# Attention: weigh and total steps placed one at a time by the planner, six slots for exponentials, and a later load of the output weights

## What is computed

```
x = x + 0.5 * ffn(layernorm(x))
x = x + attention(layernorm(x))
x = x + 0.5 * ffn(layernorm(x))

attention(X):                       # 16 heads of 32, causal, 2048 tokens, per batch of 2
    Xn = layernorm(X) * ln_g + ln_b
    Q, K, V = Xn @ Wq + bq, Xn @ Wk + bk, Xn @ Wv + bv
    scores = Q @ K.T / sqrt(32), -inf above the diagonal
    A = softmax(scores)
    return (A @ V) @ Wo + bo
```

## Time and profile before

| | us |
|---|---|
| median of 3 runs | 2569.63 (2569.61 to 2570.26) |
| the profiled execution | 2570.1 |
| its span of instructions | 2568.3 |
| TensorE busy in the span | 2478.6 (97%) |
| VectorE busy | 1770.7 (69%) |
| GpSimd busy | 1543.9 (60%) |
| ScalarE busy | 1465.2 (57%) |

### The profile page before, as it was taken

One profiled execution on the slowest core, in us unless ns is written; L12 is line 12 of the kernel. 1 busy time (PEld: TensorE's weight loads), 2 busy tenths in 40 slices (PEclk: granted clock), 3 DMA queues, 4 the chain that ended last, 5 costly groups with the idle time before them and its releaser, 6 DMA issues.

```text
span 2568.3 us, 39616 instructions
## 1 busy us (share of the span) xinstructions
PE 2478.6 (97%) x14559; PEld 1100.9 (43%) x14559; DVE 1770.7 (69%) x3016; ACT 1465.2 (57%) x2829; POOL 1543.9 (60%) x1604
## 2 busy tenths in 40 slices
PE   5899999999999999999999999999999999999998
PEld 3444444444443434333344434444333444444443
DVE  7866666667659594948486695858575866666665
ACT  6666666665225656566622256565655466666665
POOL 3467666764316767676442267676774467766775
PEclk9999999999999999999999999999999999999999
DMA  2012211121122020200231312020004301111101
GB/s 67 17 47 78 91 41 50 50 99 66 33 60 61 12 46 22 52 6 2 88 128 34 81 41 52 7 52 22 3 4 149 123 17 50 50 50 50 50 33 50
DMA packets 78017, 130.58 MB, mean 51 GB/s; under 512 B 19551, under 2 KB 24698, under 8 KB 77694
## 3 DMA queue, kind: packets, MB, share of 16 engines
q1 hardware_dynamic: 77822, 128.05, 16.2%
HBM read 68.23 MB, written 31.46 MB: 39 GB/s over the span
## 4 chain that ended last, share of the span: by engine, by line
PE 77%; POOL 6%; DVE 6%; ACT 4%; issue 2%; SPq 1%; DMA 0%; POOLq 0%; DVEq 0%; ACTq 0%
PE pp L97 59%; PE ps L97 17%; POOL sb L106 5%; ACT sb L103 4%; DVE sb L112 2%; DVE sb L118 1%; SPq L139 1%; PE ps L100 1%; POOL sb L109 1%; DVE sb L106 1%; PE pp L100 0%; DVE sb L115 0%; DMA sb<-sb 0%; DVE sb L109 0%; DVE sb L124 0%
## 5 line engine op out<-in xcount | busy, mean ns | idle before, releaser
L97 PE MATMUL pp<-sb,sb 128*128 128x512 f16 (+8 forms) x11230 | 2068.8, 420 | 32.6 <-DVE sb L112 14.4
L106 POOL TENSOR_TENSOR sb<-sb,sb 128x512 f32<-128x512 f32 (+7 forms) x1353 | 1490.9, 1127 | 993.2 <-PE pp L97 330.4
L97 PEld LDWEIGHTS pp<-sb,sb 128*128 128x128 f16 (+3 forms) x11230 | 799.8, 102 | 1068.5 <-issue 214.5
L97 PE MATMUL ps<-sb,sb 128*128 128x512 f16 (+8 forms) x2786 | 723.1, 348 | 26.8 <-DVE sb L112 13.6
L103 ACT ACTIVATE sb<-pp 128x512 f32<-128x512 f32 (+6 forms) x1035 | 521.2, 560 | 331.2 <-PE pp L97 317.3
L118 DVE TENSOR_REDUCE sb<-pp 128x1 f32<-128x512 f32 (+3 forms) x704 | 441.0, 667 | 150.2 <-PE pp L97 150.0
L103 ACT ACTIVATE sb<-sb 128x512 f16<-128x512 f32 (+4 forms) x513 | 326.0, 650 | 366.0 <-DVE sb L112 306.4
L112 DVE SCALAR_TENSOR_TENSOR sb<-pp,sb,sb 128x512 f32<-128x512 f32 x447 | 324.6, 746 | 151.5 <-PE pp L97 136.6
L112 DVE SCALAR_TENSOR_TENSOR sb<-ps,sb,sb 128x512 f32<-128x512 f32 x437 | 318.1, 747 | 154.7 <-PE ps L97 128.7
L97 PEld LDWEIGHTS ps<-sb,sb 128*128 128x128 f16 (+3 forms) x2786 | 251.3, 97 | 339.9 <-DVE sb L118 36.0
L103 ACT ACTIVATE sb<-ps 128x512 f32<-128x512 f32 (+5 forms) x473 | 262.7, 566 | 155.3 <-PE ps L97 123.2
(11 more groups left out here) (29 smaller groups left out, 373.3 us busy)
## 6 DMA issues: line engine op xcount, KB each, us to landing
sb<-sb SPq DMA_DIRECT2D x144, 128.0 KB, 2.4
sb<-L_attn_X SPq DMA_DIRECT2D x64, 256.0 KB, 3.4
sb<-xa SPq DMA_DIRECT2D x64, 256.0 KB, 4.2
sb<-xc SPq DMA_DIRECT2D x64, 256.0 KB, 3.4
xa<-sb SPq DMA_DIRECT2D x32, 256.0 KB, 2.0
xc<-sb SPq DMA_DIRECT2D x32, 256.0 KB, 4.4
out<-sb SPq DMA_DIRECT2D x32, 256.0 KB, 2.0
sb<-sb SPq DMA_DIRECT2D x48, 96.0 KB, 2.2
```

The costliest lines, as they stand in the source:

```text
L97: return self.e.matmul(*a, **k) if self.e else self
L106: return self.e.tensor_tensor(*a, **k) if self.e else self
```

## The change

The block of three is given up. The 240 weigh and total steps still come in one fixed sequence (weigh 0, weigh 1, then weigh k, total k-1, weigh k+1 for each even k), but each is a candidate of its own, and the planner tracks whether the array was last used by f16 matmuls ("row") or by 32-column ones ("col"). From "row" a weigh or total costs 100 ns and a penalty of 300 ns less a fifth of VectorE's backlog; from "col" it costs only its waits, less 0.11 of the smaller backlog of VectorE and ScalarE. The weights of the other costs change as well, among them that of max units by their lead. Scores may run 11 heads ahead of the next weigh (15 once no max unit is left), and those beyond eight get a penalty of 300 ns.

Slots are no longer counted round. `pick` takes the known slot that is released first: four slots up to step 15, six from step 16 (two new ones at C0 and C0 + 8192, where the projected keys of head groups 0 and 1 lay, free once these are stacked), and from step 120 the same six as before. An even step's slot is free after its pair's total, as before; an odd step's slot is free once its exponentials are weighed and added, head by head.

The load of Wo comes right behind total 119 (the C0 slots are in use until then), with a wait for it on SyncE's queue, and `wo_split` starts after step (3, 1, 4), n = 128. The rule by which additions go to VectorE is the same in effect (the first clause of `late`, four steps after the last rows; the second can't be true with its 1e9), and is now kept as a set.

```diff
 class Att: __init__
-        self.E = [... for x in [o + 8192 * i for i in range(NE)] + [QS0 + 98304, QS0 + 106496]]
+        self.E = [... for x in [o + 8192 * i for i in range(NE)] + [QS0 + 98304, QS0 + 106496, C0, C0 + 8192]]
-    def place(self, n):
-        ...
 order
-        m = 0
-        while m < N:
+        m, hold = 0, [None] * 8
+        def released(k):
+            if k is None:
+                return 0.0
+            if k % 2:
+                return max(added[k], weigh_end[k]) if k in added else None
+            return sum_end.get(k + 1)
+        def pick(n):
+            most = range(NE) if n < 16 else (0, 1, 2, 3, 6, 7) if n < 120 else range(6)
+            known = [(released(hold[i]), i) for i in most if released(hold[i]) is not None]
+            return min(known) if known else None
+        late, mode, where = False, "row", 0
+        line = [x for k in range(0, N, 2) for x in
+                [("total", k - 1) if x == "T" else ("weigh", k + int(x)) for x in '0T1'] if x[1] >= 0]
+        while line:
...
-            if ready and 4 * n + j < 4 * m + 8 + (4 if wide else 4):
+            if ready and 4 * n + j < 4 * m + 8 + (7 if wide else 3):
-                cand.append((max(pe, clear[i], rowed[steps[n][0:2]]) + 0.200000 * hunger + (0 if first else 0.000000), "score", i))
+                cand.append((max(pe, clear[i], rowed[steps[n][0:2]]) + 0.050000 * hunger + (0 if first else 300.000000), "score", i))
-                    hunger = max(dve - pe, 0) + 10000.000000 * (lead - 0.080000)
-                    cand.append((max(pe, clear[i]) + 0.200000 * hunger, "max", i))
+                    hunger = max(dve - pe, 0) + 6272.000000 * (lead - 0.096000)
+                    cand.append((max(pe, clear[i]) + 0.050000 * hunger, "max", i))
...
-            if n >= m + 2 and (m == 0 or m - 1 in added):
-                ...
-                cand.append((pe + idle + 2500.000000 - 1.000000 * min(max(dve - pe, 0), 2000), "stay", 0))
+            op, k = line[0]
+            can = k in added if op == "total" else 4 * n + j >= 4 * k + 4
+            if can:
+                ok = (max(added[k], inverted if steps[k][2] == 1 else 0.0) if op == "total" else
+                      max(exped[k, 3], kept if steps[k][2] == 0 else 0.0))
+                begin = max(ok, pe + (100.000000 if mode == "row" else 0))
+                cand.append((begin + (300.000000 - 0.200000 * min(max(dve - pe, 0), 2000) - 0.000000 * min(max(act - pe, 0), 2000)
+                                      if mode == "row" else
+                                      0.000000 - 0.110000 * min(max(min(dve, act) - pe, 0), 2000)), "stay", 0))
...
             if what == "stay":
-                seq = [("total", m - 1) if x == "T" else ("weigh", m + int(x)) for x in '0T1']
-                m += 2
+                seq = [line.pop(0)]
+                if op == "weigh":
+                    m = k + 1
+                elif k == 119:
+                    seq.append(("wo", None))
+                if mode == "row":
+                    pe += 100.000000
+                mode = "col"
...
-                      if steps[n] == (2, 1, 0):
-                          out.append(("wo",))
-                      if steps[n] == (2, 3, 0):
+                      if steps[n] == (3, 1, 4):
                           parts.extend(("wo_split", c) for c in range(KC))
 att_act, score
-            elif m >= 0:
-                e.wait_ge(*t.sum_done.at((b, m + 1 - m % 2)))
+            elif m % 2 == 0:
+                e.wait_ge(*t.sum_done.at((b, m + 1)))
             else:
+                e.wait_ge(*t.av_done.at((b, m)))
+                e.wait_ge(*(t.late_added.at((b, m, j // 2)) if m in t.late[b] else t.e_added.at((b, m, j))))
 att_sp, wo
+            e.wait_ge(*t.sum_done.at((b, 119)))
```

More of the change, by code:

```diff
@@ L1324, in __init__ @@
         self.banks = [Banks() for _ in range(B)]
-        self.late = [0] * B
+        self.late = [set() for _ in range(B)]
+        self.slots = {}
         self.late_added = p.sign("a_late_added")
         self.plan = [list(self.order(b)) for b in range(B)]
-    def place(self, n):
[L1331 to L1335, removed]
     def offset(self, n):
@@ L1418, in order @@
         total_units, total_scores = len(units), 4 * N
-        m = 0
-        while m < N:
+        m, hold = 0, [None] * 8
[13 more added lines that the diff above has]
+        while line:
             n, j = scored
-            slot = self.place(n)[1] if n < N else None
-            free = slot is None or slot < 0 or slot + 1 - slot % 2 in sum_end
+            free = n < N and (j or pick(n))
             wide = not units
@@ L1474, in order @@
                   pe = at + c / 2.4 + 3 + (57 if kt >= 4 * qt else 0)
-                  place, old = self.place(n)
-                  free = sum_end.get(old + 1 - old % 2, 0.0) if old is not None and old >= 0 else 0.0
+                  if j == 0:
+                      gone, slot = pick(n)
+                      self.slots[n] = slot, hold[slot]
+                      hold[slot] = n
+                  free = gone
                   act = max(act, pe + 235, free) + 0.833 * c + 52
@@ L1521, in order @@
                   out.append(ev)
+              elif what == "wo":
+                  out.append(("wo",))
               elif what == "weigh":
@@ L1529, in order @@
                   if n % 2:
+                      work, start = 4 * c, max(weigh_end[n - 1], exped[n, 3])
+                      if late and n >= late or max(dve, start) + 1.04 * work + 1000000000.000000 < max(pool, start) + 2.117 * work:
+                          self.late[b].add(n)
                       for h in range(4):
                           start = max(weigh_end[n - 1], exped[n, h])
-                          if self.late[b] and n >= self.late[b]:
+                          if n in self.late[b]:
                               dve = max(dve, start) + 1.04 * c + 32
@@ L1549, in order @@
                       inverted = max(dve, sum_end[n]) + 745
-        self.sum_up(out, parts, N - 1)
+        for k in range(N - 2 + 1, N, 2):
+            self.sum_up(out, parts, k)
         yield from out
@@ L1665, in att_pe @@
                 e.wait_ge(*t.inverted.at((b, *t.steps[n - 2][0:2], 0)))
-            e.wait_ge(*(t.late_added.at((b, n, 1)) if n >= t.late[b] else t.e_added.at((b, n, 3))))
+            e.wait_ge(*(t.late_added.at((b, n, 1)) if n in t.late[b] else t.e_added.at((b, n, 3))))
             for j in range(4):
-                k = e.matmul(RS[32 * j:32 * j + 32, off:512], p.ones[:, :], t.E[t.place(n - 1)[0]][:, j, off:512],
+                k = e.matmul(RS[32 * j:32 * j + 32, off:512], p.ones[:, :], t.E[t.slots[n - 1][0]][:, j, off:512],
                              start=kt == 1, stop=last)
@@ L1752, in att_dve @@
             n = at[0]
-            if n % 2 and n >= t.late[b]:
+            if n in t.late[b]:
                 add_steps(e, p, b, n, t.late_added)
@@ L1799, in att_pool @@
             n = at[0]
-            if n % 2 and n < t.late[b]:
+            if n % 2 and n not in t.late[b]:
                 add_steps(e, p, b, n, t.e_added, 1)
```

43 lines of the change are left out of this document (18 added, 25 removed).

## The result

The changed kernel takes 2537.95 us, the median of 4 runs (2537.59 to 2538.51), against 2569.95 us for the kernel before on the same chip: 32 us less, ratio 0.9874 with a 95% interval of 0.9857 to 0.9892. The forecast was 2540 us.

A forecast was written before the change was run, and what follows sets the result against it. TensorE, busy 97%, was taken as the bound, with 44 us of waits in each 504 us loop. Gains 6 + 11 - 5 + 0 + 2 + 1 = 15 us a batch, twice 30, gave 2570.1 - 30 = 2540 us; range 2512 to 2567.

The forecast's parts named there:

- 6 + 11 + 2 + 1: Attention loops, us gained a batch: 6 six slots, 11 single steps, 2 Wo's split, 1 start and last rows.
- second kind: Stretches with max units: full banks make loads wait, about 17 us a batch; single steps were to remove 11.
- first kind: Stretches without max units: weighs wait for their own exponentials, about 13 us a batch; six slots were to gain 6.
- GpSimd as next limit: Stretches without max units: GpSimd's four additions a pair, 4.96 us, hold the period at about 5.0 us, not 4.60.
- 105 blocks at 0.20 us: Attention loops: 25 more 32-column blocks a batch than 80, each 0.20 us for changing form, 5 us lost.
- the ends (0.10 to 0.33): Bounds in us on the price of changing to 32-column form and back, taken as 0.20.
- The estimate of 0.33 us a block: Price of a 32-column block by the Trainium skill's 166 ns latency; 25 blocks would cost 8 us, not 5.
- 2 of 6 us were to go: ScalarE's copies for the splits: 6 us of waits a batch, 2 covered by exponentials up to eleven heads ahead.
- waits go nearly whole: Rival, attention loops: slots and single steps fill each full bank, 27 us a batch gained, 2516 us; chance 0.17.
- Slots waiting for GpSimd in place of the total: Rival, stretches without max units: period stays 5.48 us, gain only 7 us a batch, 2556 us; chance 0.18.
- VectorE as the true bound: Rival, stretches with max units: VectorE bounds, savings return as changes of form, no measurable change, 2570 us; chance 0.05.
- Slower by changes of form, from 180 blocks on: Rival, attention loops: from 180 blocks a batch the change loses; at 240 blocks 2594 us; chance 0.08.

The follow-up runs named there:

- singles: Single steps with the changed kernel's cost weights, but four slots up to step 120 and early Wo load as in the kernel before; 2552.46 us.
- wolate: The kernel before with only the late load of Wo and its late split; 2575.74 us, ratio 1.0018 to the kernel before.
- oddtotal: The changed kernel, but odd steps' slots also wait for their pair's total, six slots kept; 2537.15 us, 148 blocks a batch.
- pen150: The changed kernel with the planner's penalty for leaving f16 matmuls at 150 ns instead of 300; 2604.45 us, 184 blocks.
- pen1000: The changed kernel with the planner's penalty for leaving f16 matmuls at 1000 ns instead of 300; 2949.23 us, 107 blocks.
- lowlate: The changed kernel with GpSimd's eight subtractions for the splits moved to steps 148 to 155; 2537.45 us, ratio 0.9872 to the kernel before.

## Why the prediction was right, step by step

**The place and the sum.** The loops were to shrink by 15 us a batch; between the same two matmuls they shrank by 16.5 and 16.3 us. TensorE's records stayed in number. The place, the kinds of gain and loss and the next limit were right. That the sum came out right to 2 us is luck in part, because two errors in it met: 10 us too few of waits gone, 10 us too few for blocks.

**The waits.** Forecast were 20 us of 44 gone a batch (6 + 11 + 2 + 1); 30 went. The term of the second kind was too small. I gave single steps 11 of 17 us and left them nothing of the first kind; singles shows that they take 27 us with four slots, blocks without max units included. A block of three had to wait for its last exponential in line, while single steps let TensorE score in between. So the two parts overlap, and the split of the gain by kinds (6 for slots, 11 for steps) doesn't hold. The slots' own share was 4 us a batch in blocks of three, and on top of single steps 5 (16 blocks and 1 us of waits).

**GpSimd as next limit.** This held. In the stretch without max units:

```profile
994.34 18.41 POOL L106 TENSOR_TENSOR sb<-sb,sb 128x512 f32<-128x512 f32 x15
```

15 additions in 18.41 us without a gap are 4.91 us a pair, the "about 5.0" of the forecast.

**The blocks.** I had 105 blocks at 0.20 us, 5 us; there are 143 at 0.24, 15 us. The number failed in its second half: I read two steps a block with max units and three or more without. The order has 64 blocks of one step, 64 of two and 15 longer; those with max units close by hold 1.5 steps, the others 2.4. The backlog that keeps TensorE in "col" is the smaller of two, and I had reckoned with VectorE's 1.5 us alone. That was the step: with VectorE's backlog alone in the rule the planner writes 113 blocks, and with the term taken out it writes the same 143, so ScalarE's backlog leaves nothing of it. The price lay within the ends (0.10 to 0.33): the step was to take the change from load starts on one side only, 0.10 us, where the block's own side has 0.14. The Trainium skill says in "TensorEngine Tiling (Array Packing)", Key Properties, that changing the tiling mode drains TensorE. The trace agrees in so far as each change has its price; that it is a drain no run here shows. The estimate of 0.33 us a block, from the 166 ns of the Trainium skill's "TensorE: Matmul & The Clock Gate", Single matmul latency, was too high against 0.24 measured.

**Wo.** Too low in the changed kernel, and wrong in sign by itself. 2 of 6 us were to go; the splits cost 0.85 + 1.98 us, against 2.9 + 1.2 + 2.3 before, so that 3.6 went. There the exponentials that are ahead do cover part of the copies, as argued, and 2.8 us of gain a batch come with the place, by the table above. In blocks of three the same move loses 2.6 us a batch (wolate), so the gain hangs on the other parts. That no load and no queue is held up by the late DMA was right.

**The rivals.** That waits go nearly whole came true for the waits and not for the time, since blocks paid for it. Slots waiting for GpSimd in place of the total: refuted: the period is 4.91 us and not 5.48, and oddtotal shows that it makes no difference by which the slot is freed. VectorE as the true bound: refuted, the same 359 us of it stand in 485. Slower by changes of form, from 180 blocks on: pen150 with 184 is slower by 1.3%, but of the 66 us that it lost to the changed kernel blocks are only 20; the rest is waits, over half of them for rows that come too late. For the mechanism as told, the threshold would lie higher: 30 us of waits pay for 125 blocks at 0.24 us beyond the 80 of before.

**Open.** What the new cost weights do apart from the single steps. And why early release of odd slots is worth nothing, when the order has 5 blocks more without it: 1.2 us a batch were expected from these alone and 0.8 us in all was measured, the other way and within the scatter. In batch 0 oddtotal has 1.4 us less of waits in the first sixty weighs and totals, which is about what its blocks cost; why its order waits less there no run shows.

## What to carry to other kernels

When one engine is 97% busy, compare the starts of its instructions with their arithmetic before you believe the 97%: 44 of 504 us were waits here. A planned order that can leave a wait for another kind of work gains those, but count what each change costs from undisturbed blocks on both sides of the change, and keep what is far off in time (rows, DMAs) early: one penalty in a greedy planner controlled both, and moving it either way lost more than the whole gain. And work put into a shared order for one engine stands in the queues of the others too: a subtraction that waits for a late copy stopped additions, totals and TensorE in turn.

## What the runs showed of the hardware

A 32-column f32 block between f16 matmuls costs 0.24 us beyond its columns, the same for one step as for three. The granted clock fell to 1.2 GHz behind long waits of TensorE (0.67 in 974 to 993 us of pen1000, where it took one max unit each 0.6 us), so that a wait costs more than its length.

It doesn't fall each time. In the changed kernel TensorE's loads stand 1.21 and 0.96 us in front of the first scores of tile 2 in batch 0, and 1.27 and 0.96 us in batch 1, but in the loops the clock fell only once, in batch 1. In lowlate, with the same order, it fell at this place in both batches. The changed kernel's two batches and lowlate's first:

```profile
800.00:812.00 12.00, 10.16 (x81) 3.90 (x78) 10.12 (x18) 6.13 (x14) 2.47 (x5) 1.00 0.04 10
1480.00:1492.00 12.00, 10.11 (x58) 3.63 (x50) 9.04 (x16) 6.10 (x11) 2.31 (x5) 0.86 0.03 9
798.00:810.00 12.00, 10.16 (x74) 4.04 (x71) 9.99 (x17) 6.17 (x14) 1.88 (x5) 0.86 0.04 10
```

Counted with all around them, the waits here are 2.9 us without the fall and 3.9, 4.1 and 4.2 us with it: up to 1.3 us more for the same work. So two executions of one order differ here by the clock and not by the DMAs, whose 3.12 us from issue to first score are the same in all (in lowlate from 801.82 to 804.94 us). One fixed figure in the planner fits them.
